# Layer 1's exponentials, norms and turned weights in another order; layer 3's end as products with diagonal matrices, and one product per chunk in place of four

## The reference

```
# layer 1: s = causal softmax(q k / sqrt(32)) v ;  f = for each token its best of 8 experts, all computed
probs = softmax(xn @ router_w + router_b); y = max(probs) * (xn @ expert_w[argmax] + expert_b[argmax])
# layer 3, s: a recurrence over 8 chunks of 64 tokens, M a 128x128 state per batch
outputs = chunk @ M.T ;  h = silu(outputs @ vg_w1.T) @ vg_w2.T + outputs ;  v_target = h.mean(tokens)
M_new   = decayed M + rate * (v_target - M k_mean) k_mean^T, gated, its norm held under 30
s       = silu(outs @ vg_w1.T) @ vg_w2.T + outs
# layer 3, f: each token's two best of 8 experts, weighted, plus a shared expert
f = sum_k w_k * square(relu(xn @ w_fc[e_k].T)) @ w_proj[e_k].T + shared(xn)
```

## Time and profile before

| | |
|---|---|
| median of 3 runs | 1404.84 us (1404.35 to 1404.96) |
| profiled execution: its time, its span | 1417.23 us, 1415.5 us |
| TensorE products, busy | 1155.0 us (82%) |
| VectorE busy | 997.0 us (70%) |
| ScalarE busy | 761.7 us (54%) |
| GpSimd busy | 615.9 us (44%) |
| layer 1, about | 573 to 724 us of the span |
| layer 3, about | 1200 us to the end |

### The profile page before, as it was taken

How to read it: one execution, slowest core, us unless ns; L and a number is a source line. 1 busy time by engine, 2 the same in 40 slices (tenths; PEclk the granted TensorE clock), 3 DMA queues, 4 the chain that set the end, 5 groups by cost and what they waited for, 6 DMA issues and landing times. The chain is left out here.

```text
span 1415.5 us, 21028 instructions
## 1 busy us (share of the span) xinstructions
PE 1155.0 (82%) x7010; PEld 812.6 (57%) x7010; DVE 997.0 (70%) x2280; ACT 761.7 (54%) x1584; POOL 615.9 (44%) x607
## 2 busy tenths in 40 slices
PE   3999999998888786377966887888887778988885
PEld 1455665664564575266844555555555555777774
DVE  2476677669787654567737989989989997634445
ACT  1456556555545445244437686586767674344442
POOL 3244444544348824443101533633633753136661
PEclk9999999999999898588978998998999999789997
DMA  7400000000000033810000000000000000001113
GB/s 174 117 1 1 1 1 1 1 1 1 1 8 24 30 89 102 253 35 16 1 12 0 1 1 1 1 1 0 1 1 1 1 1 14 18 17 39 40 38 105
DMA packets 54443, 40.71 MB, mean 29 GB/s; under 512 B 13185, under 2 KB 46687, under 8 KB 54337
## 3 DMA queue, kind: packets, MB, share of 16 engines
q1 hardware_dynamic: 40994, 27.58, 6.8%
q0 software_dynamic: 4544, 9.32, 2.4%
q10 hardware_dynamic: 8800, 2.48, 0.9%
HBM read 26.32 MB, written 13.04 MB: 28 GB/s over the span
## 5 line engine op out<-in xcount | busy, mean ns | idle before, releaser
L780 POOL TENSOR_TENSOR PR<-PR,R 128x512 f32<-128x512 f32 (+3 forms) x128 | 160.6, 1266 | 231.7 <-DVE R L1275 231.2
L1980 POOL TENSOR_TENSOR YY<-YY,H 128x512 f32<-128x512 f32 x120 | 164.3, 1392 | 187.6 <-DVE H L2430 187.6
L410 PE MATMUL banks<-XT,we 128*128 128x128 f32 (+1 forms) x568 | 175.2, 440 | 11.9 <-ACT HH L2252 10.5
L1074 ACT ACTIVATE PR<-banks,NM 128x257 f32<-128x257 f32 (+3 forms) x256 | 132.4, 527 | 94.8 <-DVE NM L1247 93.0
L410 PEld LDWEIGHTS banks<-we,HH 128*128 128x128 f32 x1024 | 145.1, 205 | 35.4 <-issue 30.2
L2422 DVE TENSOR_TENSOR_SCAN H<-wide,H 128x1024 f32<-128x1024 f32 x64 | 164.4, 2568 | 0.2
L410 PE MATMUL banks<-we,HH 128*128 128x128 f32 x1024 | 145.5, 289 | 0.0
L410 PE MATMUL banks<-BCR,SEL 96*128 96x512 f32 x128 | 68.2, 535 | 76.4 <-DVE H L2430 65.1
L2252 ACT ACTIVATE HH<-banks,be1f 128x512 f32<-128x512 f32 x128 | 84.1, 687 | 83.5 <-PE banks L410 82.6
L410 PEld LDWEIGHTS banks<-XT,we 128*128 128x128 f32 x568 | 90.4, 202 | 65.3 <-issue 43.4
L410 PEld LDWEIGHTS banks<-PTS,V 128*64 128x64 f32 x1152 | 66.4, 139 | 84.1 <-issue 53.7
(11 more groups left out here) (564 smaller groups left out, 2447.5 us busy)
## 6 DMA issues: line engine op xcount, KB each, us to landing
xsort<-zrow SPq DMA_DIRECT2D x1, 3072.0 KB, 13.9
XS<-xsort SPq DMA_DIRECT2D x12, 256.0 KB, 2.9
ysort<-PTS SPq DMA_DIRECT2D x12, 256.0 KB, 2.2
pj_stage<-in_L_ffn_w_proj SPq DMA_DIRECT2D x1, 2048.0 KB, 12.0
we<-in_L_ffn_we SPq DMA_DIRECT2D x1, 2048.0 KB
we<-yrows SPq DMA_DIRECT2D x8, 256.0 KB, 5.4
xrows<-XN SPq DMA_DIRECT2D x4, 256.0 KB, 3.5
out<-XN SPq DMA_DIRECT2D x4, 256.0 KB, 2.3
```

The costliest lines, as they stand in the source:

```text
L410: return nc.tensor.matmul(o, l, r, start=start, stop=stop)
L780: last = nc.gpsimd.tensor_tensor(p, p, R[:, T * q + t, :].unsqueeze(2).to_broadcast([P, 2, w]), ALU.mult)
L1074: nc.scalar.activation(PR0[:, q % 2, s, OFF[t]:OFF[t] + w], ps2(n)[:, s, SLOT[t]:SLOT[t] + w], ACT.Exp, bias=NM[:, m, s:s + 1], accum_out= ...
L1980: nc.gpsimd.tensor_tensor(YY[:, m, :], YY[:, m, :] if n else XD[m], H[:, k % 4, m, :], ALU.add).then_inc(ya, 1)
```

## The change

In layer 1 six of the 18 turns are moved to the end of round 0, and three stand in each round after; the fourth and fifth places of a round go. On ScalarE, exponentials 2 and 3 come ahead of the stores of the attention output, and the copies of round 0's turns stand between and behind the exponentials. On VectorE `choose` moves behind `add_expert(b, 6)` and `apply_in(j + 1)`, and a wait for the weights is added ahead of `add_expert(b, 0)`.

In layer 3 HAZ gets one group of 32 columns per chunk with four columns that are not zero, and one product takes the place of four. At the end VectorE makes 32 diagonal matrices DG of 128x128 (eight operations, in the room of the first expert matrices fcT), one for each weight column. TensorE puts ACC into banks 0 to 3 by products with the unit matrix and adds the products of DG and YB onto it; ScalarE takes silu from there. `final` has a bank of its own for each batch (4 to 7), SA3 and its copies go, and VectorE reads s from PSUM.

```
-                TURNS = [(), range(0, 4), range(4, 8), range(8, 12), range(12, 18)]
+                TURNS = [range(0, 6), range(6, 9), range(9, 12), range(12, 15), range(15, 18)]
 # TensorE, end of a round
                                 expert(b, 5)
-                                turn(TURNS[j][3:4])
                                 expert(b, 6)
-                                turn(TURNS[j][4:])
                                 expert(b, 7)
+                            else:
+                                turn(TURNS[0])
 # ScalarE
                                 exps(j, 1)
+                            if not back:
+                                store_turned(TURNS[0][0:1])
+                            if front:
+                                exps(j, 2)
+                            if not back:
+                                store_turned(TURNS[0][1:2])
+                            if front:
+                                exps(j, 3)
                             if back:
                                 store_s(b, 2)
                                 store_s(b, 3)
-                                store_turned(TURNS[j][3:4])
-                            if front:
-                                exps(j, 2)
-                                exps(j, 3)
                             if more:
                                 gate_next(j + 1)
                             if back:
-                                store_turned(TURNS[j][4:])
                                 gate(b)
+                            else:
+                                store_turned(TURNS[0][2:])
 # VectorE
                                 inverse(b)
+                                v.wait_ge(wgs, b + 1)
                                 add_expert(b, 0)
...
                                 stats_in(j + 1)
-                            if front:
-                                choose(j)
                             if back:
                                 add_expert(b, 6)
                             if more:
                                 apply_in(j + 1)
+                            if front:
+                                choose(j)
                             if back:
                                 add_expert(b, 7)
 # layer 3, TensorE
                                 pe.wait_ge(ha, k + 1)
-                                for b in range(B):
-                                    m = b * NC + k
-                                    last = mm(PS[0:NM, 7, 0:P], HAZ[:, m * NM:(m + 1) * NM], vg2m[:, :], start=False, stop=b == B - 1)
-                                last.then_inc(er, 1)
+                                mm(PS[0:NM, 7, 0:P], HAZ[:, k, :], vg2m[:, :], start=False, stop=True).then_inc(er, 1)
...
                         for b in range(B):
                             final(b)
+                        pe.wait_ge(ac, B - SH)
+                        pe.wait_ge(re_, NS)
+                        pe.wait_ge(oe, NS)
+                        for b in range(B):
+                            for t in range(T):
+                                mm(PS[:, b, t * P:(t + 1) * P], ident[:, :], ACC[:, b, t, :], start=t == 0, stop=False)
+                        for b in range(B):
+                            pe.wait_ge(dg, b + 1)
+                            pe.wait_ge(yl[b], 32)
+                            for t in range(T):
+                                for k in range(2):
+                                    last = mm(PS[:, b, t * P:(t + 1) * P], DG[:, k, b * T + t, :], YB[:, b, k, t, :], start=False,
+                                              stop=t == T - 1 and k == 1)
+                            last.then_inc(ad, 1)
 # layer 3, ScalarE
-                            nc.scalar.activation(SA3[:, b % 2, :, :].rearrange(flat), PS[:, 6 + b % 2, :], ACT.Copy).then_inc(fos, 1)
                             act.wait_ge(ad, b + 1)
-                            nc.scalar.activation(GS[:, b % 2, :, :], ACC[:, b, :, :], ACT.Silu).then_inc(gt, 1)
+                            nc.scalar.activation(GS[:, b % 2, :, :].rearrange(flat), PS[:, b, :], ACT.Silu).then_inc(gt, 1)
 # layer 3, VectorE
-                        def combine(b):
...
+                        v.wait_ge(wf, NS)
+                        for b in range(B):
+                            for k in range(2):
+                                last = nc.vector.tensor_tensor(DG[:, k, b * T:(b + 1) * T, :],
+                                                               ident[:, :].unsqueeze(1).to_broadcast([P, T, P]),
+                                                               WK3[:, k, b * T:(b + 1) * T].unsqueeze(2).to_broadcast([P, T, P]),
+                                                               ALU.mult)
+                            last.then_inc(dg, 1)
+                        for b in range(B):
+                            v.wait_ge(gt, b + 1)
+                            v.wait_ge(fo, b + 1)
+                            gate_and_add(link, GS[:, b % 2, :, :], PS[:, 4 + b, :].rearrange("p (t d) -> p t d", t=T),
+                                         X4[:, b, :, :], XN4[:, b, :, :]).then_inc(done, 1)
```

More of the change, by code:

```diff
@@ L2597, in layer3 @@
             nq, nn, nrm, srt = (lsem(f"a3_{k}") for k in ("squares", "norm_sum", "norm_stored", "norm_root"))
-            fo, fos, done = (lsem(f"a3_{k}") for k in ("final", "final_stored", "output"))
+            fo, done, dg = (lsem(f"a3_{k}") for k in ("final", "output", "diagonals"))
             shifted, expd = lsem("f3_shifted"), lsem("f3_expd")
@@ L2655, in layer3 @@
                 DXZ = sbr("DXZ", [P, NM * NM], c=c)
-                HAZ = sbr("HAZ", [P, NM * NM], c=c)
+                HAZ = sbr("HAZ", [P, NC, NM], c=c)
                 vg2m = sbr("vg2m", [P, P], c=c)
@@ L2664, in layer3 @@
                 NR = sbr("NR", [P, NC, B], c=c)
-                SA3 = sbr("SA3", [P, 2, T, D], c=c)
                 GS = sbr("GS3", [P, 2, T, D], c=c)
@@ L2676, in layer3 @@
                 HS = we2[:, 4:8, :, :].rearrange("p e c d -> p e (c d)")
+                DG = fcT[:, 0:E, :].rearrange("p e (i q) -> p (e i) q", q=P).rearrange("p (k m) q -> p k m q", k=2)
                 YB = we1[:, :, :].rearrange("p (b k) (t d) -> p b k t d", k=2, t=T)
@@ L2729, in _ @@
                         nc.gpsimd.tensor_tensor(NSQ[:, :], NSQ[:, :], half16[:, :], ALU.pow).then_inc(ns, 1)
-                        nc.gpsimd.memset(HAZ[:, :], 0.0).then_inc(zeroed, 1)
+                        nc.gpsimd.memset(HAZ[:, :, :], 0.0).then_inc(zeroed, 1)
                         nc.gpsimd.tensor_copy(N[:, :, :], M0T[:, :].unsqueeze(1).to_broadcast([P, B, P])).then_inc(zeroed, 1)
@@ L2837, in final @@
                             pe.wait_ge(hs, NC)
-                            if b >= 2:
-                                pe.wait_ge(fos, b - 1)
                             for t in range(T):
-                                o = PS[:, 6 + b % 2, t * P:(t + 1) * P]
+                                o = PS[:, 4 + b, t * P:(t + 1) * P]
                                 mm(o, HS[:, b, t * P:(t + 1) * P], vg2T[:, :], start=True, stop=False)
@@ L2993, in _ @@
                         for b in range(B):
-                            act.wait_ge(fo, b + 1)
                             if b >= 2:
                                 act.wait_ge(done, b - 1)
-                            nc.scalar.activation(SA3[:, b % 2, :, :].rearrange(flat), PS[:, 6 + b % 2, :], ACT.Copy).then_inc(fos, 1)
                             act.wait_ge(ad, b + 1)
-                            nc.scalar.activation(GS[:, b % 2, :, :], ACC[:, b, :, :], ACT.Silu).then_inc(gt, 1)
+                            nc.scalar.activation(GS[:, b % 2, :, :].rearrange(flat), PS[:, b, :], ACT.Silu).then_inc(gt, 1)
                     @block.vector
@@ L3165, in _ @@
                                     v.wait_ge(zeroed, 4)
-                                nc.vector.reduce_sum(HAZ[:, (NM + 1) * k:(NM + 1) * (k + (B - 1) * NC) + 1:(NM + 1) * NC],
+                                nc.vector.reduce_sum(HAZ[:, k, k:k + (B - 1) * NC + 1:NC],
                                                      HS[:, :, k * CH:(k + 1) * CH], AX.X).then_inc(ha, 1)
@@ L3196, in _ @@
                                 step(s)
-                        def combine(b):
-                            v.wait_ge(yl[b], 32)
-                            if b >= SH:
-                                v.wait_ge(ac, b - SH + 1)
+                        v.wait_ge(wf, NS)
+                        for b in range(B):
                             for k in range(2):
-                                for t in range(T):
-                                    last = nc.vector.scalar_tensor_tensor(ACC[:, b, t, :], YB[:, b, k, t, :],
-                                                                          WK3[:, k, b * T + t:b * T + t + 1],
-                                                                          ACC[:, b, t, :], ALU.mult, ALU.add)
-                                if k == 0:
```

(18 more changed lines are left out.)

## The result

| | before | after |
|---|---|---|
| median of 5 runs each, same chip | 1404.96 us (1404.35 to 1409.43) | 1398.11 us (1397.13 to 1399.09) |
| ratio after / before | | 0.9943, 95% interval 0.9927 to 0.996 |
| profiled execution: time, span | 1417.23, 1415.5 | 1398.11, 1396.3 |
| start of the last copy of an expert's product to the last addition's end | 22.43 | 19.97 |
| a chunk of layer 3, mean period of the sum into HAZ | 17.01 | 14.20 |

Forecast were 9.7 us and 1395.1; measured are 6.85 us and 1398.11, inside the range. The profiled execution of after is one of the five runs, their median; that of before took 12.4 us more than the median of its first three runs. The two profiled executions differ by 19 us, nearly three times what the runs differ by. So the two traces can't simply be subtracted; that is the first thing that the experiments had to clear up.

The account below looks back on a forecast made before the run. The prediction took VectorE's queue to bound the run's end. Gains of 2.5 + 1.4 + 3.4 + 0.4 + 2.0 = 9.7 us off the median 1404.84 gave 1395.1 us, range 1390.5 to 1400.5.

Parts of the forecast that it names:

- The end of layer 3: Run's end: weighted sums move from VectorE to TensorE's diagonal products, last addition at 1410.2 against 1412.75, 2.5 us gained.
- Rival (c): End of layer 3: TensorE's clock falls to 1.2 GHz, 10 us more, 1405.1, no change; chance 0.05.
- The lower bound of 0.4: End of layer 3: at most about 0.4 us below the forecast end, as the last rows allow 1404 + 1.8 + 2.3.
- rival (b): End of layer 3: VectorE's eight products hold up the last scatter, loads come late, 3.0 us lost, 1398.1; chance 0.09.
- One factor per chunk: Layer 3's recurrence: one product replaces four in each of 7 chunks, 1.4 us gained in all.
- The term 0.2 per chunk: Layer 3's recurrence: expected gain per chunk, 0.2 us, the middle of the two nearest readings, 0 and 0.37.
- rival (d): More than forecast: unnamed waits shrink, TensorE keeps its clock; chunks 2.6 to 4.7, layer 1 up to 8: 1390; chance 0.09.
- The 0.37 at ScalarE's copy of weights: Layer 3's chunks: ScalarE's copy of the expert's weights is next late, so at most 0.37 of 0.67 us passes.
- Layer 1: Layer 1's reordering: 3.4 us from batches 1 and 2, 0.4 from the first, 2.0 from the last; 5.8 gained.
- The first batch's 0.4: Layer 1's first batch: six turns at its end, norm ahead of the choice; 0.4 us taken between -0.8 and +1.5.
- Rival (a): Layer 1: the turned order gives nothing, GpSimd's gathers pin the phases; gain 1 instead of 5.8 us, 1399.9; chance 0.12.
- rival (e): Layer 1's first turn waits for layer 3's first weights, each microsecond after 592 lost; 1415 if they land at 612; chance 0.03.

Follow-up runs that it names:

- e1_before: The kernel before, unchanged, run again for a second trace; median 1407.15 us, ratio to before 0.9988.
- e1_layer1: The kernel before with only layer 1's part of the change; median 1402.68 us, ratio to before 0.9967.
- the delayed kernels: The changed kernel with three or six extra VectorE fills ahead of layer 2's first statistics; 1419.10 and 1421.93 us, kernel before 1422.13 on that chip.

## Why the prediction was right, and where it wasn't

The forecast of the time was right, and each of its three parts does shorten its own stage by the mechanism that was named. The sizes of two parts and the account of the whole were not right, and that the total came out near is in part luck.

*The end of layer 3* (2.5): right, in each step. 80 products in a row, 18.0 us for 17.9; clock 1.00; silu from PSUM 0.60; the multiplication with the PSUM operand 0.69; last addition 19.97 after the last copy, in all six traces with the diagonals for every batch, where 22.43 stood: 2.46 gained (1.7 to 2.5 against the other traces of the old end). Rival (c), the clock falling, didn't come; its price had been summed too low, for 56 products at 0.45 end at 1420.5 where the queue was to end at 1408.1, which is 12.4 and not 10. The lower bound of 0.4 doesn't follow from its own numbers either: 1404 + 1.8 + 2.3 is 1408.1, 2.1 under the forecast end. Of rival (b) something came, but small: the last scatter lasts 1.44 on GpSimd instead of the 0.97 of the one before it, 1.43 to 1.44 in all seven traces with diagonals, and 0.97 in the seven traces that don't. That is 0.47 more, less than one product (4.89/8 = 0.61), and the slack ahead of batch 3 took it. The Trainium skill, "SBUF — State Buffer", "Who interferes with whom", says that a VectorE instruction with two inputs in SBUF contends with a GpSimd instruction that reads SBUF, but not with one that only writes it. It says too that the shared ports are held for a whole instruction, and infers that the writing of a DMA's descriptors isn't touched by such an operation. The trace agrees with a hold of one instruction at most, and not with one for all eight; what of the scatter's issue was held, no run here shows.

*One factor per chunk* (1.4): the mechanism was right and the size wrong. The term 0.2 per chunk is the step that failed: it is 0.67 on chips A and B (14.87 to 14.20; 4.7 over the seven chunks, the upper bound and rival (d)) and about 0 on chip C, the lower bound. The mistake was to take a middle between two ends that each hold on a chip of its own. It was read from an execution whose chunks are 17.01 apart, and the other traces with four products a chunk have 14.87 on chips A and B. The 0.37 at ScalarE's copy of weights, the inner bound, held nowhere: with 0.67 gained, that copy held nothing up.

*Layer 1* (5.8): 7.6 by the gates. Batches 0 and 1 together at gate 0: 3.3 for 2.1; to gate 1: 2.4 for 1.7; to gate 2: 0.9 lost for 0; last: 2.75 for 2.0. The first batch's 0.4 came, though not at its silu, which is at 23.8 to 24.1 in five traces of the change, 22.8 in two, and 23.9 in e1_before. It came behind it, where the norm is applied ahead of the choice: the next batch's turned features (L1637) are at 30.89 in e1_layer1 and at 31.31 in e1_before, on the same chip. The six turns went as worked out, 1.8 together for each (1.11 on TensorE and then 0.69 until the copy frees the bank), and counted from the layer's start the last copy ends at 29.3 in after, for 29.6 forecast. The table load is 4.5 earlier and not 2.7; the norm waits 0.47 for GpSimd, as said. So the step that was too small is batch 1's: 2.9 at gate 0 instead of 1.7. The exponentials' order and the turns were worked out as one stall of 1.83 us; why all parts together give 3.3 at gate 0, where each alone gives 1.5, 0.1 and -0.7, isn't shown. Rival (a) falls, rival (e) too: no engine waited for the weights.

*The sum.* The terms came to 7.6 + 4.7 + (1.7 to 2.5), or 14.0 to 14.8, on chips A and B, some five more than forecast. Chip D shows as much in its time (14.1). In the first measurement (6.85) and on chip B (8.8) 5 to 8 of it are missing. About 4 of that are given back in layer 2, as chip A shows (487.5 with layer 1's change, 483.2 to 483.5 without). No term of the prediction stands for that: it took unchanged layers as unchanged in time. The rest is not accounted for, and single traces can't do it: the trace of after is 10.9 us shorter than that of e1_before, of which 3.6 lie in the opening of layer 3, which goes with the granted clock, and the trace of the changed kernel on chip D lacks these 3.6 and is the slowest of its six runs. So the forecast of 9.7 lies near the mean of the three by two errors that cancel: terms that were too small, and a loss that wasn't in it. That is luck, and on chip C, where only the delayed kernels were run, little of the gain is left. Whether the loss in layer 2 is absent on chip D wasn't seen: no trace of the kernel before was taken there, and the one of after shows the same 487.5.

## What to carry to other kernels

Before a wait without a named source enters a sum, look whether the profiled execution's own time agrees with the runs; one that is 0.9% longer may hold a stall that the runs don't have, and a term that leans on it has two values, not a middle. Layer 2, with nothing changed in it, moved here by 4 to 6 us either way between two traces; so judge a part by its own stage's length, and the whole by many runs on more than one chip. Read the granted clock of a stage beside its length before calling a difference the change's. The work that was handed from the engine at the end of the chain to one with a gapless queue was forecast here by counting, to 0.1 us over 80 products.

## What the runs showed of the hardware

- One kernel's executions differ by 1% on one chip, and the faster ones mostly have the higher mean granted clock: the changed kernel on chip B took 1389.91 us at 0.929 and 1404.58 at 0.913, on chip D 1390.47 at 0.931 and 1401.22 at 0.915.
- The same 265 records of TensorE at the opening of layer 3 take 54.5 us at a granted clock of 0.73 and 47.2 at 0.85, and the stretch lasts 62.4 and 57.4.
- Chips differ: the kernel before takes 1404.9 to 1409.0 us on A, B and D, and 1422.1 on C. In the trace of C (span 1415.7 beside 1407.2 on A) 7.9 of the 8.5 us are in layer 3, where the engines that wait for TensorE's products start some 2 us later. The first profile, 12.4 us over the median, shows the same pattern; on which chip it was taken isn't known.
- The same instructions of layer 2 last 479.4 to 489.5 us in kernels that differ only ahead of it, and 480.0 and 483.5 in two traces of one kernel; with a delay of 2.0 us ahead of them they lasted 4.1 less, though on another chip.
- A scatter issued by GpSimd beside VectorE's products with both inputs in SBUF lasts 1.44 us instead of 0.97 (seven traces of seven).
- A product of 128x128 in fp32 takes 0.2235 us in a gapless row at a granted clock of 1.00. A multiplication of 128x512 on VectorE takes 0.69 with one input in PSUM as with both in SBUF.
